# A decoder kernel: keys and values of layer 2 as three rounded products, with the low parts of the value weight in DRAM

## The chip, the cores and the metric

The kernel runs on one core of a Trainium2 chip. The metric is the device time of one execution in microseconds. A core has five engines that run side by side and wait for one another on semaphores: TensorE (PE; its weight loads are shown apart as PEld), VectorE (DVE), ScalarE (ACT), GpSimd (POOL) and SyncE (SP), which here only starts DMA transfers. Matmul results land in the eight banks of PSUM, everything else in SBUF.

## What is computed

A gated decoder of two layers on four batches of 512 rows by 512 columns. Each layer attends to a context and then runs a feed-forward part, and each part is added to the running `x` through a gate. The change touches two lines of the second layer's attention:

```python
def _L1_xattn_ref(x, cond, mask, wq, bq, wk, bk, wv, bv, wo, bo):   # 16 heads of 32
    q = _w8a8_linear(x, wq, bq)          # x and wq rounded to whole numbers up to 127
    k = cond @ wk.T + bk                 # float32, not rounded
    v = cond @ wv.T + bv                 # float32, not rounded
    attn = softmax(q k^T / sqrt(32) + mask)
    return _w8a8_linear(attn v, wo, bo)
# then: x + tanh(g) * that, and a feed-forward part (512 -> 2048 -> 512) with rounded operands
```

## The kernel before

The kernel is written engine by engine: each engine has its own list of instructions in program order, and every wait is written out. No scheduler moves anything. Layer 1 ends at about 347 us of the span, and layer 2 is the rest. Layer 2 works on one batch at a time, and all 512 rows of a batch at once: a tile is 128 rows by 512 columns, so a matrix of 512 x 512 is four tiles, and a product of two such matrices is 16 matmuls.

**Before batch 0.** TensorE turns the four weight matrices of the attention (L1393, L1400). ScalarE and VectorE copy them out of PSUM as `wqT`, `wkT` (L1255, ScalarE), `woT` (L1643) and `wvT` (L1649, VectorE). TensorE turns batch 0's context (`context`, L1420), ScalarE copies it to `ctxT` (`turned_context`, L1262), and `keys` (L1429) and `values` (L1439) multiply it by `wkT` and `wvT` as float32. Beside them VectorE normalises and rounds batch 0's rows (`query_rows`, from L57), which becomes the queries (L1455).

**High and low parts.** Scores are made from keys and queries that are each split into a rounded part and its rest: ScalarE writes `k_hi` (`key_highs`, L1267), VectorE `k_lo` (`key_lows`, L1678), and the same for `q_hi` and `q_lo` (L1297, L1721). Tiles of type F32R hold such parts. The parts are then stacked by DMA along the partitions into `k4` and `q4` (`stack_keys`, L1185, and `stack_queries`, L1196; 16 transfers for the keys of a batch, 32 for the queries). One matmul per head and row tile then gives a score (L1462). Batch 0 has transfers of its own: SP stacks the first keys (L1216), the other keys (L1222) and the last half of the queries (L1229), one after the other in SP's program; GpSimd stacks the first two quarters of the queries (L1169).

**Attention** (`attend`) goes over 64 units, a head by a row tile each, in 78 steps `s`. VectorE masks a score (L1732), ScalarE takes the exponential (L1322), TensorE turns the result (L1494), VectorE (even units) or ScalarE (odd units) copies it to `probsT` (L1762, L1313), and TensorE multiplies it by the values (L1511). `probsT` lies over the tiles that the key and query parts were made in. So the copy of unit 8, the first of the second group of eight, waits on VectorE for all stacking transfers of this batch: `k_stacked` and `q_stacked[1]`.

**The tail of a batch** is what follows the attention, and the next batch's keys and values are made in it. In program order TensorE runs: the next batch's context turned (in the last steps of the attention), two tiles of keys, the output product (L1580), two tiles of keys, three tiles of values, the turned queries, the last tile of values, the turned rows of the feed-forward part (L1410), the queries (L1455), the up product in four row tiles (L1537, each after a small matmul `hold`, L1527) and the down product (L1567). VectorE runs the row scales and rounding (L1670, L1658), the four `key_lows` between the steps of two normalisations, the values' bias (L1684), the rounding of the feed-forward rows (L1658 again), the query scaling and lows, and the hidden rows' scales. `hact`, the hidden rows that ScalarE writes (L1335), lies over `k_hi` and `k_lo`. So ScalarE waits for `k_stacked` of the next batch before it writes the first of them. Batch 3's tail has no next batch.

**Memory.** `q4` is 32 KB per partition for 16 heads; its last 8 KB are heads 12 to 15. `arena`, 32 KB, holds in turn the key parts, `ctxT`, `probsT`, `hact` and `hqT`.

## Time and profile before

| | us |
|---|---|
| median of 3 executions | 1018.43 |
| lowest and highest | 1016.8 and 1020.0 |
| the profiled execution, its own time | 1016.46 |
| its span | 1014.7 |

| engine | busy us | share of the span |
|---|---|---|
| TensorE | 899.2 | 89% |
| VectorE | 673.4 | 66% |
| ScalarE | 573.6 | 57% |
| TensorE's weight loads | 587.9 | 58% |
| GpSimd | 86.9 | 9% |

A profile is one execution seen by the hardware profiler. The span runs from the first instruction to the last. Times in the rows below are microseconds from the span's start, unless a column says ns. "SPq" is SyncE's queue issuing transfers. PEclk is the clock that TensorE was granted, as a share of 2.4 GHz; 0.5 is 1.2 GHz. The "chain of waits" is followed back from the last instruction, at each step to what released it. A float32 matmul appears as two MATMUL records, an F32R matmul as one. Records of consecutive matmuls overlap, so the pace of a stream is read from the distance of starts.

### The profile page before, as it was taken

What the parts mean: (1) busy time and instruction counts of PE and PEld (TensorE: products, weight loads), DVE (VectorE), ACT (ScalarE), POOL (GpSimd) and SP (SyncE); (2) the same over time, 40 slices, a digit from 0 to 9 for tenths busy, and PEclk for the clock granted to TensorE, in tenths of its full rate; (3) what the DMA queues carried; (4) which work ended last, traced back from release to release, by engine and by line L of the source; (5) the groups of instructions that cost most, each with busy time, mean ns of one, the idle gap of its engine ahead of it and who ended that gap; (6) DMA issues with size and microseconds to landing.
All of it is one profiled execution on the core that took longest, in us unless ns stands there. A gap on an engine that the chain in (4) does not pass through costs nothing.

```text
span 1014.7 us, 15824 instructions
## 1 busy us (share of the span) xinstructions
PE 899.2 (89%) x5592; PEld 587.9 (58%) x5592; DVE 673.4 (66%) x1870; ACT 573.6 (57%) x1094; POOL 86.9 (9%) x105
## 2 busy tenths in 40 slices
PE   3989998999999787899999999999999899999467
PEld 2868765676767453666444666445666444666233
DVE  5895860524250073798777898777798776799564
ACT  4545233355553132788347788357788447789153
POOL 2000213021120005100100000100000100000100
PEclk9999999999999999799999999999999999999769
DMA  6444556452450059510199110198110188100001
GB/s 195 141 142 159 196 205 228 146 164 86 135 198 1 23 164 197 115 43 2 42 182 191 43 43 2 42 180 186 51 43 1 43 175 196 46 2 1 1 1 42
DMA packets 52270, 102.82 MB, mean 101 GB/s; under 512 B 8924, under 2 KB 8924, under 8 KB 50656
## 3 DMA queue, kind: packets, MB, share of 16 engines
q1 hardware_dynamic: 39872, 71.88, 27.1%
q10 hardware_dynamic: 8160, 17.31, 5.1%
q0 software_dynamic: 4160, 12.62, 4.0%
q8 instruction: 45, 0.74, 0.3%
q14 instruction: 33, 0.27, 0.1%
HBM read 55.62 MB, written 14.75 MB: 69 GB/s over the span
## 4 chain that ended last, share of the span: by engine, by line
PE 36%; DVE 9%; issue 6%; ACT 5%; SPq 4%; DMA 3%; POOL 1%; POOLq 0%; DVEq 0%; ACTq 0%
PE psum L1494 7%; PE psum L1462 6%; PE psum L1567 5%; PE psum L1511 5%; PE psum L1537 5%; SPq L1185 4%; ACT probs L1322 3%; DMA k<-k_lo 3%; PE psum L1429 1%; PE psum L1553 1%; PE psum L1520 1%; DVE amax L1670 1%; DVE xn L1842 1%; DVE stats L1837 1%; DVE xn L1658 1%
## 5 line engine op out<-in xcount | busy, mean ns | idle before, releaser
L1322 ACT ACTIVATE probs<-psum,neg_max 128x512 f32<-128x512 f32 x256 | 175.0, 692 | 46.5 <-DVE neg_max L1732 46.5
L1732 DVE CUSTOM_DVE_ANT_0 psum<-psum,m_in 128x512 f32<-128x512 f32 x256 | 174.0, 703 | 18.3 <-issue 18.3
L1494 PE MATMUL psum<-ident,probs 128*128 128x128 f32 x1024 | 154.2, 275 | 0.0
L1494 PEld LDWEIGHTS psum<-ident,probs 128*128 128x128 f32 x1024 | 127.8, 141 | 19.8 <-issue 2.6
L1462 PE MATMUL psum<-k,q 128*128 128x512 f32 x256 | 125.7, 496 | 15.3 <-ACT probs L1322 6.8
L674 PE MATMUL psum<-w_sb,hT 128*128 128x512 f32 x256 | 117.6, 604 | 5.6 <-ACT hT L566 5.6
L1762 DVE COPY probsT<-psum 128x512 f32<-128x512 f32 x128 | 87.8, 686 | 2.7 <-PE psum L1494 2.5
L1313 ACT COPY probsT<-psum 128x512 f32<-128x512 f32 x128 | 75.3, 588 | 20.3 <-PE psum L1494 20.3
L594 PE MATMUL psum<-xselT_hi,w_hi 128*128 128x256 f32 x256 | 81.8, 320 | 1.6 <-ACT xselT_hi L501 1.6
L674 PEld LDWEIGHTS psum<-w_sb,hT 128*128 128x128 f32 x256 | 47.0, 192 | 55.3 <-issue 48.5
L1462 PEld LDWEIGHTS psum<-k,q 128*128 128x128 f32 x256 | 49.1, 192 | 51.7 <-ACT probs L1322 31.5
L1511 PE MATMUL psum<-probsT,vv 128*32 128x256 f32 x1024 | 68.5, 384 | 9.7 <-issue 6.1
L595 PE MATMUL psum<-xselT_lo,w_hi 128*128 128x256 f32 x256 | 71.9, 281 | 0.0
L596 PE MATMUL psum<-xselT_hi,w_lo 128*128 128x256 f32 x256 | 71.8, 281 | 0.0
L566 ACT ACTIVATE hT<-psum,b_col 128x256 f32<-128x256 f32 x64 | 26.9, 471 | 69.1 <-PE psum L596 66.5
L1162 POOL TENSOR_TENSOR xres<-xres,xn 128x512 f32<-128x512 f32 x16 | 19.8, 1268 | 531.6 <-DVE xn L1842 531.6
L1537 PE MATMUL psum<-bw1T,qxT 128*128 128x512 fp8e4 x256 | 64.4, 405 | 0.0
L1567 PE MATMUL psum<-bw2T,hqT 128*128 128x512 fp8e4 x256 | 57.1, 379 | 0.0
L1429 PE MATMUL psum<-ctxT,wkT 128*128 128x512 f32 x128 | 56.2, 593 | 0.9 <-ACT ctxT L1262 0.9
L1439 PE MATMUL psum<-wvT,ctxT 128*128 128x512 f32 x128 | 56.2, 593 | 0.0
L1335 ACT ACTIVATE hact<-psum,h_unit 128x512 f32<-128x512 f32 x64 | 41.8, 693 | 19.9 <-PE psum L1537 11.0
L594 PEld LDWEIGHTS psum<-xselT_hi,w_hi 128*128 128x128 f32 x256 | 48.3, 189 | 7.6 <-issue 5.7
(221 smaller groups left out, 1566.7 us busy)
## 6 DMA issues: line engine op xcount, KB each, us to landing
bw_raw<-in_L_ffn_W_dram ACTq DMA_DIRECT2D x16, 1024.0 KB, 5.3
c_in<-in_ctx_dram SPq DMA_DIRECT2D x8, 1024.0 KB, 5.5
k<-k_hi SPq DMA_DIRECT2D x24, 256.0 KB, 5.9
k<-k_lo SPq DMA_DIRECT2D x24, 256.0 KB, 6.7
q<-q_hi SPq DMA_DIRECT2D x48, 128.0 KB, 3.9
q<-q_lo SPq DMA_DIRECT2D x48, 128.0 KB, 3.4
xres<-in_x_dram SPq DMA_DIRECT2D x4, 1024.0 KB, 5.9
w_raw<-in_L_ffn_w_dram POOLq DMA_DIRECT2D x4, 1024.0 KB, 5.4
```

The source lines that it names most:

```text
L594: pe.matmul(dst, l_hi, r_hi, start=start, stop=False)
L595: pe.matmul(dst, l_hi, r_lo, start=False, stop=False)
L674: mm = pe.matmul(psum[j][:, :], hT[:, f % RING, j * P:(j + 1) * P], w2_sb[:, f, :], start=(f == 0), stop=(f == FT - 1))
L1313: act.copy(probsT[:, (hg + 1) % 2, r, :, (nt % 2) * P:(nt % 2) * P + P], turn_bank(u)[:, :].rearrange("p (l n) -> p l n", l=T)).then_inc(p ...
L1322: act.activation(probs[:, u % 4, :], psum[u % SCORE_BANKS][:, :], ACT.Exp, scale=-1.0, bias=neg_max[:, u:u + 1], accum_out=prob_sum[:, nt, ...
L1462: pe.matmul(psum[u % SCORE_BANKS][:, :], q4[:, h, nt * P:(nt + 1) * P], k4[:, h, :], start=True, stop=True).then_inc(score_psum, 1)
L1494: mm = pe.transpose(turn_bank(u)[:, l * P:(l + 1) * P], probs[:, u % 4, l * P:(l + 1) * P], ident[:, :])
L1511: mm = pe.matmul(psum[6 + hg % 2][HD * r:HD * (r + 1), 0:HALF], vv[:, l, h * HD:(h + 1) * HD], probsT[:, (hg + 1) % 2, r, l, :], start=(l ...
L1537: mm = pe.matmul(psum[2 + f][:, :], qxT[:, c, t * P:(t + 1) * P], bw1T[:, c, 512 * f:512 * f + 512], start=(c == 0), stop=(c == CT_ - 1))
L1567: mm = pe.matmul(psum[6 + t % 2][:, :], hqT[:, t % 2, f, :], bw2T[:, f, :], start=(f == 0), stop=(f == FT - 1))
L1732: dve.tensor_tensor_reduce(bank[:, :], bank[:, :], m_in[:, nt, :], -1.0, LOWEST, ALU.add, ALU.min, neg_max[:, u:u + 1]).then_inc(masked_re ...
L1762: dve.tensor_copy(probsT[:, (hg + 1) % 2, r, :, (nt % 2) * P:(nt % 2) * P + P], turn_bank(u)[:, :].rearrange("p (l n) -> p l n", l=T)).the ...
```

## The change

Four things are done in layer 2.

1. Context, key weight and value weight are kept as a high part of type F32R and a low part (the rest, also F32R). Each float32 matmul of `keys` and `values` becomes three F32R matmuls: high by high, high by low, low by high. ScalarE's copies now write the high parts, and VectorE subtracts them from PSUM to get the low parts: eight subtractions for the weights (where it copied `wvT` in four), and `context_lows`, four for each batch's context. ScalarE takes over the four copies of the value weight.
2. `keys` waits for the low parts too.
3. There is no room for the value weight's low part beside everything else. It is made in the last 8 KB of `q4`, stored once to DRAM (`wv_low`, 1 MB) by SP, and loaded into the same place by SP in each later batch, behind the load of `x_in`. The stacking of the second half of the queries, which writes over it, now waits for the batch's values (`v_psum`), and for the store in batch 0.
4. `attnT` and `sx_row` share 2 KB, and batch 0's context is loaded to another place.

The diff, cut to its core:

```diff
-        wkT = sb("wkT", [P, CT_, C])
-        wvT = sb("wvT", [P, CT_, C])
+        wkT_hi = sb("wkT_hi", [P, CT_, C], F32R)
+        wkT_lo = sb("wkT_lo", [P, CT_, C], F32R)
+        wvT_hi = sb("wvT_hi", [P, CT_, C], F32R)
+        wvT_lo = at("wvT_lo", [P, CT_, C], F32R, q4_at + 24 * K)
...
-        ctxT = at("ctxT2", [P, CT_, S], F32, arena + 24 * K)
+        ctxT_hi = at("ctxT2_hi", [P, CT_, S], F32R, arena + 24 * K)
+        ctxT_lo = at("ctxT2_lo", [P, CT_, S], F32R, arena + 16 * K)
...
@@ stack_queries, sync @@
+                        if half:
+                            sp.wait_ge(v_psum, b * T + T)
...
+                sp.wait_ge(linear_dve_ready, 3 * CT_)
+                sp.dma_start(wv_low, wvT_lo[:, :, :].bitcast(F32)).then_inc(wv_low_stored, 16)
                 sp.wait_ge(k_hi_ready, 1)
...
                 sp.wait_ge(q_lo_ready, CT_)
+                sp.wait_ge(v_psum, T)
+                sp.wait_ge(wv_low_stored, 16)
...
                     sp.dma_start(x_in[:, :, :], tiles(sh.x_mid[b + 1])).then_inc(x_loaded, 16)
+                    sp.dma_start(wvT_lo[:, :, :].bitcast(F32), wv_low).then_inc(wv_low_loaded, 16)
                     stack_keys(b + 1)
@@ scalar @@
-                    act.copy(wkT[:, c, :], psum[c][:, :]).then_inc(linear_act_ready, 1)
+                    act.copy(wkT_hi[:, c, :], psum[c][:, :]).then_inc(linear_act_ready, 1)
+                for c in range(CT_):
+                    act.wait_ge(linear_psum, 3 * CT_ + c + 1)
+                    act.copy(wvT_hi[:, c, :], psum[4 + c][:, :]).then_inc(linear_act_ready, 1)
@@ tensor @@
+                def three(dst, left, right, start, stop):
+                    (l_hi, l_lo), (r_hi, r_lo) = left, right
+                    pe.matmul(dst, l_hi, r_hi, start=start, stop=False)
+                    pe.matmul(dst, l_hi, r_lo, start=False, stop=False)
+                    return pe.matmul(dst, l_lo, r_hi, start=False, stop=stop)
...
-                    pe.wait_ge(ctxT_ready, b * CT_ + CT_)
+                    pe.wait_ge(ctxT_hi_ready, b * CT_ + CT_)
+                    pe.wait_ge(ctxT_lo_ready, b * CT_ + CT_)
...
-                            mm = pe.matmul(psum[4 + o][:, :], wkT[:, c, o * P:(o + 1) * P], ctxT[:, c, :],
-                                           start=(c == 0), stop=(c == CT_ - 1))
+                            mm = three(psum[4 + o][:, :], [w[:, c, o * P:(o + 1) * P] for w in (wkT_hi, wkT_lo)],
+                                       [x[:, c, :] for x in (ctxT_hi, ctxT_lo)], c == 0, c == CT_ - 1)
...
@@ vector @@
+                def context_lows(b):
+                    for c in range(CT_):
+                        dve.wait_ge(ctxT_hi_ready, b * CT_ + c + 1)
+                        dve.tensor_tensor(ctxT_lo[:, c, :], psum[CONTEXT_BANKS[c]][:, :], ctxT_hi[:, c, :].bitcast(F32),
+                                          ALU.subtract).then_inc(ctxT_lo_ready, 1)
...
                     for s in range(STEPS):
+                        if more and s == UNITS + LAG + 2:
+                            context_lows(b + 1)
...
+                context_lows(0)
                 query_rows(0, link)
```

VectorE's program before batch 0, in the kernel before. `stats` is the first step of batch 0's row normalisation.

```order
L1643 COPY woT<-psum 128x512 [waits linear_psum] x4
L1644 MEMSET turn_col 128x1
L1645 MEMSET low_col 128x1
L1646 TENSOR_SCALAR swq_col<-w_scale 128x4
L1649 COPY wvT<-psum 128x512 [waits linear_psum] x4
L1651 MEMSET held 128x1
L1652 MEMSET held 128x1
L57 BN_STATS stats<-x_in_3109 128x6 [waits x_loaded2,chain1]
```

The same place after the change.

```order
L1671 COPY woT<-psum 128x512 [waits linear_psum] x4
L1672 MEMSET turn_col 128x1
L1673 MEMSET low_col 128x1
L1674 TENSOR_SCALAR swq_col<-w_scale 128x4
L1678 TENSOR_TENSOR wkT_lo<-psum,wkT_hi 128x512 [waits linear_act_ready] x4
L1678 TENSOR_TENSOR wvT_lo<-psum,wvT_hi 128x512 [waits linear_act_ready] x4
L1681 MEMSET held 128x1
L1682 MEMSET held 128x1
L1689 TENSOR_TENSOR ctxT_lo<-psum,ctxT_hi 128x512 [waits ctxT_hi_ready2,chain1]
L1689 TENSOR_TENSOR ctxT_lo<-psum,ctxT_hi 128x512 [waits ctxT_hi_ready2] x3
L57 BN_STATS stats<-x_in_3112 128x6 [waits x_loaded2]
```

The row normalisation now stands behind the context's low parts, which wait for ScalarE's high parts.

VectorE's program in the last steps of batch 0's attention, after the change (before, the row L1689 is not there and all else is alike).

```order
L1801 COPY probsT<-psum 128x4x128 [waits pT_psum,av_psum] x2
L1807 RECIPROCAL prob_inv<-prob_sum 128x2x4 [waits probs_ready]
L1689 TENSOR_TENSOR ctxT_lo<-psum,ctxT_hi 128x512 [waits ctxT_hi_ready2] x4
L1815 TENSOR_TENSOR xn<-psum,prob_inv 128x2x128 [waits o_psum,chain2]
L1807 RECIPROCAL prob_inv<-prob_sum 128x2x4 [waits probs_ready]
L1815 TENSOR_TENSOR xn<-psum,prob_inv 128x2x128 [waits o_psum,chain2]
L1707 TENSOR_REDUCE amax<-xn 128x4 [waits o_ready]
```

The four low parts stand between the last copies of the probabilities and the last two quarters of the attention's output.

SP's program between the mask load and the first loads of batch 1, after the change. The two new transfers are L1223 and L1250; L1243 was L1229 and waited only for `q_lo_ready` and `q_hi_ready`.

```order
L1223 DMA wv_low_dram<-wvT_lo 128x2048 [waits linear_dve_ready]
L1228 DMA k_3116<-first_parts 32x512 [waits k_lo_ready,k_hi_ready]
L1228 DMA k_3116<-first_parts 32x512 x15
L1234 DMA k_3116<-k_hi_rest 32x3x512 [waits k_lo_ready,k_hi_ready]
L1234 DMA k_3116<-k_hi_rest 32x3x512 x3
L1234 DMA k_3116<-k_lo_rest 32x3x512 x4
L1234 DMA k_3116<-k_hi_rest 32x3x512 x4
L1234 DMA k_3116<-k_lo_rest 32x3x512 x4
L1243 DMA q_3117<-q_hi_rest 32x2x512 [waits v_psum,wv_low_stored,q_lo_ready,q_hi_ready]
L1243 DMA q_3117<-q_hi_rest 32x2x512 x7
L1243 DMA q_3117<-q_lo_rest 32x2x512 x8
L1185 DMA c_in_3120<-in_ctx_dram 128x4x512 [waits x_used]
L1249 DMA x_in_3112<-x_mid_dram 128x4x512 [waits ctxT_psum2]
L1250 DMA wvT_lo<-wv_low_dram 128x2048
```

The store stands ahead of all stacking transfers of batch 0, and each load behind the load of the rows.

## Rows read from the trace of the kernel before

**Rows 1.** TensorE in order of time, tail of batch 0: start us, us, operation [idle before].

```profile
486.94 7.03 PE L1429 MATMUL psum<-ctxT,wkT 128*128 128x512 f32 x16
...
507.10 10.46 PE L1439 MATMUL psum<-wvT,ctxT 128*128 128x512 f32 x24
...
522.22 1.06 PE L1410 MATMUL psum<-ident_b,xn 128*128 128x128 bf16 x16
...
534.07 0.18 PE L1527 MATMUL psum<-ident_b 128*128 128x1 bf16 x1 [3.72 <-ACT hact L1335]
```

**Rows 2.** VectorE in order of time, the same tail.

```profile
485.28 0.42 DVE L1776 TENSOR_TENSOR xn<-psum,prob_inv 128x256 f32<-128x256 f32 x1 [3.75 <-PE psum L1520]
...
487.67 2.29 DVE L1670 TENSOR_REDUCE amax<-xn 128x4 f32<-128x2048 f32 x1
...
492.92 2.46 DVE L57 BATCH_NORM_STATS2 stats<-x_in 128x6 f32<-128x512 f32 x4
...
508.02 0.75 DVE L1678 SCALAR_TENSOR_TENSOR k_lo<-psum,bk_col,k_hi 128x512 fp32r<-128x512 f32 x1
...
517.76 1.67 DVE L1658 TENSOR_SCALAR xn<-xn,inv 128x512 f32<-128x512 f32 x4
```

**Rows 3.** Queue of SP in order of time, the same tail.

```profile
483.83 0.38 SPq L1235 DMA_DIRECT2D x_in<-x_mid_dram  x1
508.85 3.54 SPq L1185 DMA_DIRECT2D k<-k_hi  x4
```

**Rows 4.** The chain of waits, the same tail: start us, us, what.

```profile
523.78 9.52 DMA k<-k_lo
...
533.33 0.70 ACT hact L1335
```

**Rows 5.** DMA issues by tile: KB of one transfer, median us from issue to landing.

```profile
x_in<-x_mid_dram SPq DMA_DIRECT2D x4, 1024.0 KB, 5.6
```

**Rows 6.** TensorE in order of time, layer 1: three-product matmuls, 24 starts apart.

```profile
60.13 0.39 PE L596 MATMUL psum<-sig_hi,ctxT_lo 128*128 128x512 f32 x1
...
65.57 0.39 PE L596 MATMUL psum<-sig_hi,ctxT_lo 128*128 128x512 f32 x1
```

**Rows 7.** VectorE, groups by line, layer 1's low parts: busy us, mean ns of one.

```profile
L824 DVE TENSOR_TENSOR ctxT_lo<-psum,ctxT_hi 128x512 fp32r<-128x512 f32 x16 | 9.9, 682 | 0.0
```

**Rows 8.** ScalarE in order of time, before batch 0's attention.

```profile
361.49 0.59 ACT L1257 COPY swo_row<-psum 128x512 f32<-128x512 f32 x1 [1.49 <-PE psum L1404]
362.82 2.05 ACT L1262 COPY ctxT<-psum 128x512 f32<-128x512 f32 x4 [0.75 <-PE psum L1420]
```

**Rows 9.** VectorE in order of time, before and in batch 0's attention.

```profile
362.16 0.69 DVE L57 BATCH_NORM_STATS2 stats<-x_in 128x6 f32<-128x512 f32 x1
...
373.74 0.74 DVE L1678 SCALAR_TENSOR_TENSOR first_parts<-psum,bk_col,first_parts 128x512 fp32r<-128x512 f32 x1
...
420.46 0.69 DVE L1762 COPY probsT<-psum 128x512 f32<-128x512 f32 x1
```

**Rows 10.** Queue of SP in order of time, before batch 0's attention.

```profile
374.55 10.14 SPq L1216 DMA_DIRECT2D k<-first_parts  x16
...
406.57 5.55 SPq L1229 DMA_DIRECT2D q<-q_lo_rest  x8
```

**Rows 11.** TensorE in order of time, batch 0's first scores.

```profile
407.57 1.62 PE L1462 MATMUL psum<-k,q 128*128 128x512 f32 x3 [6.31 <-DMA q<-first_parts]
```

**Rows 12.** Windows: start:end, length, five engines' busy us, PEclk, DMA share, GB/s.

```profile
419.00:420.00 1.00, 0.87 (x5) 0.56 (x5) 1.00 (x6) 1.00 (x4) 0.00 (x0) 1.00 0.32 59
```

**Rows 13.** Windows: the clock before and in the up products, tails of batches 0 to 2.

```profile
530.00:534.00 4.00, 0.35 (x2) 0.00 (x0) 0.23 (x1) 0.67 (x2) 0.00 (x0) 1.00 1.08 206
...
683.00:690.00 7.00, 4.73 (x18) 1.90 (x19) 4.41 (x9) 3.88 (x7) 0.00 (x0) 0.76 0.98 200
...
838.00:846.00 8.00, 7.59 (x34) 3.22 (x35) 5.77 (x10) 5.80 (x10) 0.00 (x0) 0.79 0.97 200
```

**Rows 14.** TensorE in order of time, batch 1's tail: the wait before its second up product.

```profile
685.27 0.18 PE L1527 MATMUL psum<-ident_b 128*128 128x1 bf16 x1 [2.47 <-ACT hact L1335]
```

More of the change, by code:

```diff
@@ L1071, in layer1 @@
         ctxT_psum = sem("ctxT_psum2")
[L1072 removed]
+        ctxT_hi_ready = sem("ctxT_hi_ready2")
+        ctxT_lo_ready = sem("ctxT_lo_ready2")
+        wv_low_stored = sem("wv_low_stored")
+        wv_low_loaded = sem("wv_low_loaded")
         k_psum = sem("k_psum")
@@ L1261, in turned_context @@
                         act.wait_ge(ctxT_psum, b * CT_ + c + 1)
-                        act.copy(ctxT[:, c, :], psum[CONTEXT_BANKS[c]][:, :]).then_inc(ctxT_ready, 1)
+                        act.copy(ctxT_hi[:, c, :], psum[CONTEXT_BANKS[c]][:, :]).then_inc(ctxT_hi_ready, 1)
                 def key_highs(b, tiles, k_hi=by_tile(k_hi)):
@@ L1438, in values @@
                         for c in range(CT_):
-                            mm = pe.matmul(psum[4 + t][:, :], ctxT[:, c, t * P:(t + 1) * P], wvT[:, c, :],
-                                           start=(c == 0), stop=(c == CT_ - 1))
+                            mm = three(psum[4 + t][:, :], [x[:, c, t * P:(t + 1) * P] for x in (ctxT_hi, ctxT_lo)],
+                                       [w[:, c, :] for w in (wvT_hi, wvT_lo)], c == 0, c == CT_ - 1)
                         mm.then_inc(v_psum, 1)
@@ L1646, in _ @@
                 dve.tensor_scalar(swq_col[:, :], sh.w_scale[:, 0, :], Q_SCALE, None, ALU.mult).then_inc(chain1, 1)
-                for c in range(CT_):
-                    dve.wait_ge(linear_psum, 3 * CT_ + c + 1)
-                    dve.tensor_copy(wvT[:, c, :], psum[4 + c][:, :]).then_inc(linear_dve_ready, 1)
+                for i, (w_hi, w_lo) in enumerate(((wkT_hi, wkT_lo), (wvT_hi, wvT_lo))):
+                    for c in range(CT_):
+                        dve.wait_ge(linear_act_ready, (i + 1) * CT_ + c + 1)
+                        dve.tensor_tensor(w_lo[:, c, :], psum[4 * i + c][:, :], w_hi[:, c, :].bitcast(F32),
+                                          ALU.subtract).then_inc(linear_dve_ready, 1)
                 dve.memset(held[:, 7:8], 0.0).then_inc(x_done, 1)
@@ L1653, in _ @@
                 dve.wait_ge(chain1, 3)
+                def context_lows(b):
+                    for c in range(CT_):
+                        dve.wait_ge(ctxT_hi_ready, b * CT_ + c + 1)
+                        dve.tensor_tensor(ctxT_lo[:, c, :], psum[CONTEXT_BANKS[c]][:, :], ctxT_hi[:, c, :].bitcast(F32),
+                                          ALU.subtract).then_inc(ctxT_lo_ready, 1)
                 def quantize():
@@ L1823, in batch @@
                     link.count = FIRST_LINKS
-                    attend(b, link)
+                    attend(b, link, more)
                     dve.wait_ge(o_ready, b * HG + HG)
```

20 lines of the change are left out of this document (12 added, 8 removed).

## The prediction

> **What bounds the kernel now.** I read the profile in this order: the chain of waits over layer 2, then each engine in order of time around the keys and values, then the windows with the granted clock. TensorE is the busiest engine, so less work for it looks like less time. The chain says otherwise in the places where the keys and values are made.
>
> In the tail of batch 0 VectorE starts the row scales at 487.67 [rows 2] and works without a gap that matters until the last low part of the keys at 508.02 to 508.77 [rows 2]. At 508.85 SP starts to issue the 16 key transfers [rows 3], the last of them is released at 523.78 and takes 9.52 us, and ScalarE's first hidden row starts when it has landed, at 533.33 [rows 4]. TensorE has waited 3.72 us for that by then [rows 1]. So from 487.67 to 533.33 the tail is VectorE, then SP's queue, then DMA. TensorE's matmuls lie beside them. The tails of batches 1 and 2 repeat this; batch 3's has no keys.
>
> Before batch 0 the chain does run over the keys' matmuls, but two other things stand close. VectorE normalises the rows from 362.16 and makes the first low key at 373.74 [rows 9]; SP then issues 48 stacking transfers, from 374.55 to 406.57 + 5.55 = 412.12 with hardly a gap [rows 10]. In the window 419 to 420 the DMA share falls to 0.32 [rows 12], so the last lands at about 419.3. The copy of unit 8 waits for all of them and ran at 420.46 [rows 9]. The slack is 1.2 us.
>
> **Part 1, three F32R matmuls for one float32.** Eight float32 matmuls of the keys show as 16 records; the next group starts right behind them. They took 7.03 us, about 0.87 us each [rows 1]. Layer 1 has matmuls of the same form and size, and 24 starts lie 65.57 - 60.13 = 5.44 us apart, 0.227 us each [rows 6]. A triple costs 0.68 us, so a product of 16 falls from about 13.9 to 10.9 us, and the eight products of the kernel free 24 us of TensorE.
>
> How much of it reaches the end? In a tail: the first two tiles of keys end at about 492.4 instead of 493.9. VectorE makes the first low key when it gets there, behind the rounding, and it is VectorE that is late. The second two end near 504.1, their high parts on ScalarE near 504.9, while VectorE reaches the last low key at 508.02 as before. So the transfers start at 508.85 as before. The values then end at about 516.3; the turned feed-forward rows need VectorE's rounding, 517.76 + 1.67 = 519.4 [rows 2], and start there instead of at 522.22 [rows 1]. The queries come 2.7 us earlier, and so does the first up product. All this ends in front of 533.33, which hasn't moved: TensorE waits some 6.4 us instead of 3.72. Gain of a tail: 0, bounded by 0 and the 2.7 us.
>
> A rule of the skill speaks against the exchange. The Trainium skill, in "TensorE: Matmul & The Clock Gate" under Part 3 (packing small matmuls), says that a weight load overlaps a matmul in flight only when their row groups differ. By that rule an estimate for a product is 48 x (0.227 + some 0.19 of weight load), near 20 us and dearer than before; the starts 0.227 us apart with a full-size weight load in each leave no room for it.
>
> **Part 2, low parts on VectorE.** One costs 9.9 / 16 = 0.62 us [rows 7], four of them 2.5 us. In a tail they go between VectorE's copy that ended at about 481.5 and the multiply at 485.28, where it was idle 3.75 us [rows 2]. ScalarE's four high parts end at about 484.6, so the last low part ends near 485.8 and the multiply slips 0.5 us. Its reader is the row scale at 487.67, behind a second multiply that waits for TensorE until 487.2. Cost 0; without that cover it would be 2.5 us a tail. The keys start behind a matmul at 486.94 [rows 1], later than 485.8. Cost 0.
>
> Before batch 0 there is no cover. ScalarE gets four more copies of 2.05 / 4 = 0.51 us. It was idle 1.49 us before 361.49 [rows 8], so free from 360.00, and `swo_row` moves to 362.05, 0.56 us later. The turned context waits for that PSUM bank, so the high parts of the context run from 363.38 to 365.43 [rows 8]. VectorE's low parts start at about 363.9 and end at 366.4. Only then come the row statistics, 366.4 instead of 362.16 [rows 9]: 4.25 us later. The keys end at 366.4 + 10.9 = 377.3, and VectorE arrives at the first low key at 373.74 + 4.25 = 378.0. So here too VectorE has become the later one. All four low keys are done at about 381.0, where they were done at 380.5: the queries lose 0.5 us, regain 0.7 us with the first tile of values, and the first scores [rows 11] start at 407.57 less 0.2 to 0.5.
>
> But SP's first transfer moves with the first low key, 374.55 + 4.25 = 378.8. SP is a queue with no gaps, so its last lands at 419.3 + 4.25 = 423.6. The copy of unit 8 wanted to start at 420.46; VectorE's masks queue behind it, and ScalarE and TensorE behind these. **Cost 3.1 us.** Bounds: 0, if the transfers flow faster once bunched, and 4.25 plus 1.7 for the clock after such a stop (below).
>
> **Part 3, the DRAM detour.** The store of 1 MB is issued at about 364, when SP has nothing else; it is over when the stacks start. The load goes out behind `x_in` at 483.83 [rows 3]. A transfer of that size lands 5.6 us after its issue [rows 5]: `x_in` at 489.4, needed at 492.92 [rows 2]; if the two share the engines evenly, `x_in` needs at most twice that, 495.0. Cost 0 to 2.1 us in each of three tails; I take 0, since one queue issues `x_in` first. The values need the load only at about 504. The new waits of the second half of the query stacks are for values done near 398 (batch 0) and 516 (a tail), while SP gets there at about 402 and 539. Queued behind them are the other query transfers and the mask load. Cost 0. The Trainium skill ("DMA: Bandwidth & Descriptors", on issuing engines not being separate queues) says that all transfers share the same 16 engines and interleave; by it the load could take x_in's share, which is the 2.1 us above.
>
> **Part 4, the clock.** TensorE's clock was 1.00 before the up product of batch 0's tail, after a wait of 3.72 us [rows 1, 13]. In the tail of batch 1 the wait was 2.47 us [rows 14], and the clock fell to 1.2 GHz for a while: mean 0.76 over 7 us, a loss of 0.24 x 7 = 1.7 us. The tail of batch 2 shows 0.79 over 8 us, again 1.7 us [rows 13]. TensorE bounds the up product, so this counts. After the change each tail has a wait of some 6.4 us there, and another of 3.1 us before the turned rows. I take it that batch 0's tail now loses 1.7 us like the others, and the others what they lose now: **cost 1.7 us**. Bounds: -3.4 us (no tail loses any) and +6.7 us (each loses twice 1.7).
>
> **The sum.** 1016.46 + 3.1 + 1.7 = 1021.3 us against the profiled execution. The median of the runs shown is 1018.43, 2.0 us above that execution, so for a median I say 1023.2, or 1023.
>
> **The rivals.**
> - *Neither the stacks nor the clock bite.* The transfers of batch 0 drain within the slack, the clock is as before. Nothing is on the path, the first scores gain 0.2 to 0.5 us. 1018.4, give or take 1.5. For it: the stall rests on 4.25 us against 1.2 us of slack and on a full DMA queue staying as slow.
> - *The clock bites harder.* Each tail loses 3.4 us instead of 0, 1.7, 1.7 (+6.7), and the stop in batch 0 adds 1.7 to its 3.1: 1018.4 + 11.5 = 1029.9. For it: TensorE waits twice in each tail where it waited once.
> - *Faster: the up product starts earlier.* Its place is the wait at 534.07. Were SP's key transfers or their landing bound by something that TensorE's earlier end relieves, the 2.7 us of each tail would come through: 1018.4 - 3 x 2.7 + 3.1 = 1013.4. It decides from the point where the last key transfer lands before about 527.7, when the first up product now ends. Against it: SP starts them on VectorE's last low key, at 508.85 in both.
> - *The triple is no cheaper than float32*, by the weight loads. Then a product is 6 us longer and the tails gain nothing: the keys before batch 0 end 3 us later than now, the values in a tail later too, some 12 us in all, 1030. The distance of starts [rows 6] all but excludes it.
>
> **How the numbers follow.** Forecast 0.50; rival one 0.23; harder clock 0.15; faster 0.10; dear triples 0.02. A measurement can tell about 0.3%, 3 us. The forecast's +4.8 us is over that by less than 2 us, so a fifth of its chance falls to "same", and so does part of rival one's on either side. Slower 0.40 + 0.15 + 0.02 + 0.01 = 0.58; same 0.10 + 0.20 = 0.30; faster 0.10 + 0.02 = 0.12. The range holds the forecast, rival one and most of the harder clock: 1016 to 1029.
>
> **What would show it.** VectorE's row statistics before batch 0 should start near 366.4, SP's first key transfer near 378.8, and the copy of unit 8 should wait for a DMA until about 423.6. In a tail the last low key should stand where it stood, some 21 us behind the row scales, TensorE's wait before the second up product should be about 6.4 us, and the windows there should show a clock under 1.00 in all three. If the copy of unit 8 doesn't wait, the first term is wrong; if the clock stays at 1.00, the second.

## The result, and the profile after

| | before | after |
|---|---|---|
| median of 7 executions, us | 1018.43 | 1023.9 |
| lowest and highest | 1016.8, 1021.09 | 1018.84, 1028.06 |
| the profiled execution | 1016.46 | 1021.81 |
| its span | 1014.7 | 1020.0 |

The ratio is 1.0058, with a 95% interval from 1.0039 to 1.0078: slower, by about 6 us. A second series on another chip gave 1.0068 (1.0051 to 1.0085).

The page after says that TensorE is less busy, 886.2 us instead of 899.2, and that the span is longer all the same:

```profile
PE 886.2 (87%) x5720; PEld 613.1 (60%) x5720; DVE 685.1 (67%) x1890; ACT 575.1 (56%) x1098; POOL 87.4 (9%) x105
...
PEclk9999999999999898799998999999999999999869
```

To find the place I cut layer 2 at events that both traces have, and took the differences. The times are microseconds read from the engines' rows in order of time. "Second" is a second profile of the same kernel, on another chip.

| from, to | before | second | after | second |
|---|---|---|---|---|
| layer 2's start, SP's first key transfer | 21.23 | 21.64 | 25.02 | 25.75 |
| layer 2's start, copy of unit 8 | 67.14 | 67.51 | 72.59 | 73.90 |
| copy of unit 8, row scales of batch 0's tail | 67.21 | 66.42 | 68.29 | 68.54 |
| row scales, first hidden row: tail 0 | 45.66 | 45.65 | 44.95 | 44.97 |
| the same, tail 1 | 44.40 | 44.39 | 44.40 | 44.39 |
| the same, tail 2 | 44.67 | 44.62 | 44.46 | 44.49 |
| first hidden row, next first score: tail 0 | 26.24 | 27.54 | 28.70 | 28.77 |
| the same, tail 1 | 27.91 | 27.91 | 26.25 | 26.25 |
| the same, tail 2 | 27.91 | 27.91 | 27.90 | 27.91 |
| layer 2's start, end | 656.71 | 657.52 | 662.81 | 664.53 |

The end is that of VectorE's last instruction. The attentions of batches 1 to 3 (80.6, 80.6 and 78.7 us) are equal within 0.1 us, and batch 3's tail within 0.3. So the loss lies before and in batch 0's attention: 6.5 us in the first pair and 8.5 us in the second, more than all of it in either. The three up products' stretches together are 0.8 us longer in the first pair and 0.4 us shorter in the second, so a loss there isn't shown.

**Before batch 0.** ScalarE after the change, in order of time. Columns: start us, length us, engine, line, operation, out<-in, count, [idle before <- releaser].

```profile
358.70 2.10 ACT L1273 CAST wvT_hi<-psum 128x512 fp32r<-128x512 f32 x4
360.60 0.69 ACT L1275 COPY swo_row<-psum 128x512 f32<-128x512 f32 x1
362.04 2.05 ACT L1280 CAST ctxT_hi<-psum 128x512 fp32r<-128x512 f32 x4 [0.75 <-PE psum L1445]
```

VectorE in the same place:

```profile
357.40 2.48 DVE L1678 TENSOR_TENSOR wkT_lo<-psum,wkT_hi 128x512 fp32r<-128x512 f32 x4 [0.77 <-ACT wkT_hi L1270]
359.80 2.48 DVE L1678 TENSOR_TENSOR wvT_lo<-psum,wvT_hi 128x512 fp32r<-128x512 f32 x4
...
362.72 2.49 DVE L1689 TENSOR_TENSOR ctxT_lo<-psum,ctxT_hi 128x512 fp32r<-128x512 f32 x4 [0.43 <-ACT ctxT_hi L1280]
365.12 2.46 DVE L57 BATCH_NORM_STATS2 stats<-x_in 128x6 f32<-128x512 f32 x4
...
376.71 0.75 DVE L1715 SCALAR_TENSOR_TENSOR first_parts<-psum,bk_col,first_parts 128x512 fp32r<-128x512 f32 x1
```

The four low parts (2.49 us) stand in front of the row statistics at 365.12, and they can't start before the first high part is there, at 362.72. Counted from layer 2's start (353.32 before, 352.51 after) the statistics moved from 8.84 to 12.61, the first low key from 20.42 to 24.20: 3.8 us each [rows 9], and 4.1 us in the second pair. ScalarE's four copies of the value weight, which the prediction charged with 0.56 us, moved nothing in this pair: `swo_row` starts 8.09 us behind layer 2's start instead of 8.17, and the context's high parts 9.53 instead of 9.50 [rows 8]. In the second pair `swo_row` starts 0.3 us later. SP's queue follows:

```profile
377.53 10.12 SPq L1228 DMA_DIRECT2D k<-first_parts  x16
...
412.79 5.15 SPq L1243 DMA_DIRECT2D q<-q_lo_rest  x8
```

ScalarE and VectorE at unit 8, the first in each row with the wait in brackets:

```profile
425.09 0.58 ACT L1331 COPY probsT<-psum 128x512 f32<-128x512 f32 x1 [4.70 <-DMA q<-q_lo_rest]
425.10 0.69 DVE L1801 COPY probsT<-psum 128x512 f32<-128x512 f32 x1 [5.55 <-issue]
```

The last query transfer was issued at 417.35 and landed 7.7 us later, at 425.0. ScalarE waited 4.70 us, VectorE 5.55, which before had no wait there [rows 9]. But before it was a close thing. The last query transfer in the kernel before, its issue at 411.51 and its time to landing:

```profile
L1229 SPq DMA_DIRECT2D q<-q_lo_rest x1: 599/599/599, 411.5 to 411.5; - x1
...
DMA to landing us min/median/max: 8.8/8.8/8.8
```

It landed at 420.3, 0.1 us before the copy of unit 8 at 420.46. In the second profile of the kernel before it landed at 420.45, and VectorE had to wait for it:

```profile
420.52 0.69 DVE L1762 COPY probsT<-psum 128x512 f32<-128x512 f32 x1 [0.70 <-issue]
```

So the kernel before had no slack here, and the delay of SP's queue reaches unit 8 in full. After the stop TensorE ran on a lower clock. Windows: start:end, length, busy us of TensorE, its weight loads, VectorE, ScalarE, GpSimd, then PEclk, DMA share, GB/s.

```profile
420.00:425.00 5.00, 1.97 (x15) 1.38 (x11) 0.00 (x0) 0.39 (x2) 0.00 (x0) 0.97 0.74 136
425.00:430.00 5.00, 3.75 (x21) 2.38 (x25) 4.59 (x15) 3.91 (x10) 0.00 (x0) 0.50 0.00 0
430.00:435.00 5.00, 4.65 (x36) 2.97 (x32) 3.38 (x14) 2.84 (x7) 0.00 (x0) 0.85 0.00 0
```

**In the first tail.** VectorE, then SP, ScalarE and TensorE, after the change:

```profile
488.88 2.48 DVE L1689 TENSOR_TENSOR ctxT_lo<-psum,ctxT_hi 128x512 fp32r<-128x512 f32 x4 [1.62 <-ACT ctxT_hi L1280]
491.28 0.42 DVE L1815 TENSOR_TENSOR xn<-psum,prob_inv 128x256 f32<-128x256 f32 x1
...
493.39 2.29 DVE L1707 TENSOR_REDUCE amax<-xn 128x4 f32<-128x2048 f32 x1
513.77 0.73 DVE L1715 SCALAR_TENSOR_TENSOR k_lo<-psum,bk_col,k_hi 128x512 fp32r<-128x512 f32 x1
```

```profile
489.99 1.74 SPq L1250 DMA_DIRECT2D wvT_lo<-wv_low_dram  x1
514.59 3.58 SPq L1193 DMA_DIRECT2D k<-k_hi  x4
```

```profile
510.48 0.69 ACT L1285 ACTIVATE k_hi<-psum,bk_col 128x512 fp32r<-128x512 f32 x1 [2.11 <-PE psum L1412]
...
538.34 2.42 ACT L1353 ACTIVATE hact<-psum,h_unit 128x512 f32<-128x512 f32 x4 [5.70 <-DMA k<-k_lo]
```

```profile
525.06 1.05 PE L1435 MATMUL psum<-ident_b,xn 128*128 128x128 bf16 x16 [2.04 <-DVE xn L1695]
...
539.08 0.19 PE L1555 MATMUL psum<-ident_b 128*128 128x1 bf16 x1 [5.73 <-ACT hact L1353]
```

The low parts fit into VectorE's idle time. The last high key ends at 511.17, but VectorE reaches the last low key at 513.77, 20.38 us behind the row scales; before it was 20.35 [rows 2]. TensorE has two waits now, 2.04 us for the rounded rows (none before) and 5.73 us for the first hidden row (3.72 before [rows 1]). In tails 1 and 2 the second wait is 3.51 and 3.81 us (2.47 [rows 14] and 2.74 before). There the clock falls early, behind the first of the two waits (in tail 2 once more behind the second); tail 1, TensorE behind the wait and then a window:

```profile
679.25 1.05 PE L1435 MATMUL psum<-ident_b,xn 128*128 128x128 bf16 x16 [2.03 <-DVE xn L1695]
```

```profile
681.00:684.00 3.00, 3.00 (x9) 1.04 (x8) 1.04 (x2) 1.74 (x3) 0.00 (x0) 0.50 1.07 203
```

TensorE is slower in this place but still comes before the keys' transfers, so this fall costs nothing. The DRAM load is issued behind `x_in`, and no engine waits for either.

### The profile page after: what moved, and what is told of

The parts are those of the page before. It is cut to its first block, busy times and chain, and to the rows that moved or that the text cites. A ratio compares the mean times of both kernels' runs of the same rounds, so it can differ in the third digit from the quotient of the medians.

```text
span 1020.0 us, 16116 instructions
## 1 busy us (share of the span) xinstructions
PE 886.2 (87%) x5720; PEld 613.1 (60%) x5720; DVE 685.1 (67%) x1890; ACT 575.1 (56%) x1098; POOL 87.4 (9%) x105
## 4 chain that ended last, share of the span: by engine, by line
PE 32%; DVE 11%; SPq 8%; issue 6%; ACT 5%; DMA 3%; POOL 0%; POOLq 0%; DVEq 0%; ACTq 0%
PE psum L1522 7%; PE psum L1490 6%; PE psum L1595 5%; PE psum L1539 5%; PE psum L1565 5%; SPq L1193 4%; ACT probs L1340 3%; DMA k<-k_lo 2%; SPq L1234 2%; PE psum L1581 1%; DVE amax L1707 1%; SPq L1243 1%; DVE stats L57 1%; SPq L1228 1%; PE psum L1548 1%
## 5 line engine op out<-in xcount | busy, mean ns | idle before, releaser
L1340 ACT ACTIVATION_READ_ACCUMULATOR probs<-psum,neg_max 128x1 f32 x256 | 52.5, 205 | 0.0
L595 PEld LDWEIGHTS psum<-xselT_lo,w_hi 128*128 128x128 f32 x256 | 48.2, 188 | 5.7 <-issue 5.7
```

The lines of the kernel that those rows point to most:

```text
L595: pe.matmul(dst, l_hi, r_lo, start=False, stop=False)
L1340: act.activation(probs[:, u % 4, :], psum[u % SCORE_BANKS][:, :], ACT.Exp, scale=-1.0, bias=neg_max[:, u:u + 1], accum_out=prob_sum[:, nt, ...
```

## The experiments

Every kernel was profiled. Times of segments are from layer 2's start unless said otherwise. The first four kernels below ran once each, 1025.29, 1024.16, 1022.38 and 1019.60 us, with 1021.38 us for the kernel before beside them. Single executions of the changed kernel lie between 1018.8 and 1028.1 us, so these four tell nothing by their times and are read by their segments.

### One product instead of three

```diff
-                    pe.matmul(dst, l_hi, r_hi, start=start, stop=False)
-                    pe.matmul(dst, l_hi, r_lo, start=False, stop=False)
-                    return pe.matmul(dst, l_lo, r_hi, start=False, stop=stop)
+                    return pe.matmul(dst, l_hi, r_hi, start=start, stop=stop)
```

> The changed kernel with one matmul (high by high) in place of three in all keys and values of layer 2; the low parts are still made, stored and loaded, only not multiplied, so keys and values are only as good as the high parts. TensorE does 256 matmuls of 0.23 us less, about 15 us in each of the three tails. Theory (VectorE, SP's queue and DMA bound the tails): the row scales to the first hidden row stay at 44.4 to 45.0 us in each tail, SP's first key transfer stays 25.0 us behind layer 2's start, and the execution changes only by the clock, within 3 us. Rival (TensorE's work in keys and values reaches the end): each tail gets shorter by several us, 10 us or more in all.

Measured: row scales to first hidden row: 45.00, 45.62 and 44.42 us. SP's first key transfer at 25.69, the copy of unit 8 at 73.13. VectorE and ScalarE in the first tail:

```profile
495.40 2.29 DVE L1705 TENSOR_REDUCE amax<-xn 128x4 f32<-128x2048 f32 x1
...
515.75 0.73 DVE L1713 SCALAR_TENSOR_TENSOR k_lo<-psum,bk_col,k_hi 128x512 fp32r<-128x512 f32 x1
510.00 0.69 ACT L1285 ACTIVATE k_hi<-psum,bk_col 128x512 fp32r<-128x512 f32 x1 [0.24 <-PE psum L1410]
...
540.40 2.42 ACT L1353 ACTIVATE hact<-psum,h_unit 128x512 f32<-128x512 f32 x4 [4.71 <-DMA k<-k_lo]
```

The last low key stands 20.35 us behind the row scales, as it does with three products. Tail 1 came out 0.6 us above the expected range: its last key transfer landed later after SP had started at the same place. Some 15 us of TensorE's work less in each tail brought nothing. The rival falls: TensorE's keys and values don't reach the end of a tail.

### Batch 0 without the context's low parts

```diff
-                            mm = three(psum[4 + o][:, :],
+                            mm = (three if b else one)(psum[4 + o][:, :],
...
-                context_lows(0)
                 query_rows(0, link)
```

(`one` multiplies high by high; `values` has the same edit, and `keys` of batch 0 doesn't wait for low parts.)

> The changed kernel where batch 0 alone leaves out its context's four low parts on VectorE and multiplies high by high only, so batch 0's keys and values are only as good as the high parts. Theory (VectorE's four low parts in front of batch 0's row statistics delay SP's stacking queue): SP's first key transfer comes 2.9 us earlier, 22.1 us behind layer 2's start instead of 25.0, and the copy of unit 8 some 3 us earlier, 69.6 instead of 72.6; the tails stay as they are. Rival (the stop at unit 8 comes from the DMA engines, not from SP's start): the copy of unit 8 moves by less than 1 us.

Measured: SP's first key transfer at 22.30, 2.7 us earlier, and the copy of unit 8 at 69.10, 3.5 us earlier than in the first profile of the changed kernel and 4.8 earlier than in the second. Layer 2's start to batch 0's row scales took 137.6 us, against 140.9 and 142.4 with the change and 134.4 and 133.9 without. The theory holds and the rival falls, with a reservation: the edit also takes two thirds of the matmuls out of batch 0's keys and values, so the first scores come 3.5 us earlier too. It is not the whole loss: between the first score (50.85) and the copy of unit 8 there are still 18.3 us, where the kernel before takes 12.9. The first scores come 3.4 us earlier here than in the kernel before, while SP's queue still starts 1.1 us later than there.

### Batch 0's low parts twice

```diff
                 context_lows(0)
+                for c in range(CT_):
+                    dve.tensor_tensor(xn[:, c, :], ctxT_hi[:, c, :].bitcast(F32), ctxT_hi[:, c, :].bitcast(F32), ALU.subtract)
                 query_rows(0, link)
```

> The changed kernel where VectorE does four more subtractions of the same size (into a tile that is overwritten later) behind batch 0's context low parts: 2.5 us more on VectorE before batch 0's row statistics, nothing else. Theory: SP's first key transfer at 27.5 us behind layer 2's start instead of 25.0, the copy of unit 8 at 75.1 instead of 72.6, the whole 2.5 us longer. Rival (DMA bound): the copy of unit 8 moves by less than 1 us.

Measured: SP's first key transfer at 27.61, 2.6 us later, as expected. The copy of unit 8 at 74.07, only 1.5 us later than in the first profile of the changed kernel and 0.2 later than in the second (73.90), and from there to the row scales 66.43 us instead of 68.29, so batch 0 was not longer at all (140.5 us to the row scales, against 140.9). Half of the expectation is a miss. The windows of this kernel show where the first scores went (TensorE's clock is the number before the DMA share):

```profile
376.00:381.00 5.00, 2.08 (x9) 1.31 (x8) 4.89 (x12) 0.69 (x2) 0.00 (x0) 0.92 0.01 3
381.00:386.00 5.00, 3.01 (x21) 2.63 (x22) 0.58 (x1) 2.71 (x3) 0.00 (x0) 0.50 0.44 102
386.00:391.00 5.00, 5.00 (x14) 1.79 (x13) 1.59 (x3) 1.44 (x2) 0.00 (x0) 0.55 0.45 105
```

TensorE waited 3.55 us for the last low key, then turned rows and made queries at 1.2 GHz. So the first score came at 60.06, 5.7 us later. ScalarE's wait for the transfers at unit 8 shrank to 0.88 us, and the clock didn't fall behind it. In this profile the late first scores and the stop lay over one another and weren't added. The run doesn't tell what a further delay of SP's queue costs, because the first scores moved as well.

### Without the DRAM detour

```diff
-                sp.wait_ge(linear_dve_ready, 3 * CT_)
-                sp.dma_start(wv_low, wvT_lo[:, :, :].bitcast(F32)).then_inc(wv_low_stored, 16)
...
-                    sp.dma_start(wvT_lo[:, :, :].bitcast(F32), wv_low).then_inc(wv_low_loaded, 16)
```

> The changed kernel without the store of the value weight's low part to DRAM and without the three loads; the values of batches 1 to 3 multiply by the high part a second time where they multiplied by the low part, so they are wrong and their cost is the same. Theory: the detour is hidden, all segments stay within 0.3 us apart from the clock. Rival (the load takes DMA time from the load of the rows): the row scales to the first hidden row get up to 2 us shorter in the tails.

Measured: row scales to first hidden row 44.96, 44.41 and 44.55 us, against 44.95, 44.40 and 44.46 with the detour. SP's first key transfer at 25.43, the copy of unit 8 at 72.17. In the tails the detour costs nothing. Before batch 0 the two changed profiles with the store stand at 72.60 and 73.90 at unit 8, a spread of 1.3 us, and the 72.17 here lies just under it, so a cost there is not told. The first scores were 1.9 us later here, at 56.30, ScalarE's wait at unit 8 was 2.46 us instead of 4.70, and the clock stayed at 1.00 behind it, so that it took 66.42 us to the row scales instead of 68.29.

### SP's order: high parts first

The stop and the tails have one thing in common: SP waits for the last low key before it issues anything. Half of its transfers copy high parts only.

```diff
                     sp.wait_ge(k_hi_ready, b * CT_ + CT_)
-                    sp.wait_ge(k_lo_ready, b * CT_ + CT_)
-                    for g, part in enumerate((k_hi, k_lo, k_hi, k_lo)):
+                    for g, part in ((0, k_hi), (2, k_hi), (1, k_lo), (3, k_lo)):
+                        if g == 1:
+                            sp.wait_ge(k_lo_ready, b * CT_ + CT_)
```

(and the same for batch 0's first quarter.)

> The changed kernel with one change in SP's order: of the 16 key transfers of a stack the eight that copy high parts go first and wait for the high parts alone, the eight of the low parts follow and wait for the low parts; in batch 0 (first quarter) and in the three tails. Theory (the stacks' start bounds both places, and TensorE's earlier keys were of no use because VectorE's last low key came late): in the tails SP starts when the last high key is there, 3.4 us earlier, so row scales to first hidden row about 41.5 us instead of 44.4 to 45.0; before batch 0 SP starts 18 us behind layer 2's start instead of 25, and the copy of unit 8 at 67.5 instead of 72.6. In all some 15 us less than the changed kernel, near 1008, faster than both. Rival (DMA engines bound the stacks): the tails gain under 1 us.

Measured: 1003.52 us, ratio to the kernel before 0.986 (0.983 to 0.989). It beats both kernels, and by more than the expected 1008. Row scales to first hidden row 41.11, 40.90 and 42.48 us, up stretches 26.25, 26.25 and 28.96; SP's first key transfer at 17.92, the copy of unit 8 at 67.06. In the first tail:

```profile
505.42 0.69 ACT L1287 ACTIVATE k_hi<-psum,bk_col 128x512 fp32r<-128x512 f32 x1 [2.11 <-PE psum L1414]
506.13 7.81 SPq L1194 DMA_DIRECT2D k<-k_hi  x8
508.72 0.73 DVE L1717 SCALAR_TENSOR_TENSOR k_lo<-psum,bk_col,k_hi 128x512 fp32r<-128x512 f32 x1
529.44 4.31 ACT L1355 ACTIVATE hact<-psum,h_unit 128x512 f32<-128x512 f32 x7 [1.85 <-DMA k<-k_lo]
```

SP starts at 506.13, right behind the last high key, 17.80 us behind the row scales (488.33) instead of 21.20, and no longer waits for VectorE's 508.72. Tail 1 starts at 17.80 too, tail 2 at 19.48: there TensorE ran the keys in part at 1.2 GHz (0.50 in the window 792 to 795), and the last high key came 1.7 us later. With the old order such a fall costs nothing, because VectorE's low key is later still: in tail 1 of the kernel with matmuls in the wait (below) the last high key came at the same late place, and SP started 21.2 us behind the row scales all the same.

### The same order in the kernel before

> The kernel before with the same change in SP's order. Theory: there the last high key ends at 508.0 and the last low key at 508.8, so a tail gains only 0.8 us, and batch 0, where unit 8 did not wait, gains nothing: some 2 us in all. Rival (the order by itself is the gain, whatever TensorE does): as much as in the changed kernel.

The edit is the one above, made in the kernel before. Measured: 1009.12 us, ratio 0.992 (0.990 to 0.994). The expected 2 us were too few. Row scales to first hidden row 43.94, 43.18 and 43.33 us, 1.2 to 1.7 less each; the copy of unit 8 at 66.18, 1 us less.

```profile
509.31 0.69 ACT L1269 ACTIVATE k_hi<-psum,bk_col 128x512 fp32r<-128x512 f32 x1 [2.75 <-PE psum L1431]
510.03 7.83 SPq L1186 DMA_DIRECT2D k<-k_hi  x8
510.03 0.75 DVE L1680 SCALAR_TENSOR_TENSOR k_lo<-psum,bk_col,k_hi 128x512 fp32r<-128x512 f32 x1
```

The start moved as forecast, from 21.2 to 20.3 us behind the row scales in each tail. Another 0.4 to 0.9 us came after it: from SP's first key transfer to the first hidden row it took 23.60, 22.85 and 23.00 us instead of 24.48, 23.23 and 23.5. What I left out is the clock. The waits before the second up product are 2.01, 1.26 and 1.40 us here instead of 3.72, 2.47 and 2.74, and all three up stretches ran at full clock in this profile (26.25, 26.25 and 26.24 us), 3.3 us less than in the first profile of the kernel before.

On top of the new order the change itself is now worth 1009.1 - 1003.5 = 5.6 us by the medians of four executions each (1008.4 to 1011.0 and 1001.2 to 1006.5). In the tails SP waits for the last high key, and that one hangs on TensorE's product: SP starts 20.3 us behind the row scales with float32 keys and 17.8 us with the three rounded products (19.5 in one tail of three). Here the cheaper product comes through.

### The new order in batch 0 alone

> The changed kernel with the new order of SP for batch 0's first quarter alone. Theory: the copy of unit 8 at 67.5 us behind layer 2's start instead of 72.6, no stop, and with it no lower clock behind it; tails as in the changed kernel. 5 to 6 us less than the changed kernel, level with the kernel before within 2 us.

Measured: 1017.10 us, ratio to the kernel before 0.9995 (0.998 to 1.001). SP's first key transfer at 17.06, the copy of unit 8 at 68.55, 1 us later than expected, with 0.77 us of waiting on VectorE instead of 5.55. From there it took 66.42 us to the row scales, the clock at 1.00; tails 45.00, 44.46 and 45.78. The changed kernel's two series stand 0.6% and 0.7% above the kernel before, so this took back the 6 to 7 us. The loss of the change is in batch 0, and it hangs on when SP's queue starts. (SP starts here even earlier than in the kernel before, whose unit 8 gained 1 us from the same order. So the time alone doesn't say that the loss is gone to the last microsecond.)

### Matmuls in TensorE's wait

```diff
                     up(b, 0, more)
+                    if more:
+                        for i in range(20):
+                            pe.matmul(psum[0][:, :], qxT[:, 0, 0:P], woT[:, 0, :], start=True, stop=True)
                     up(b, 1)
```

> The changed kernel with 20 matmuls more in each of the three tails, of which nobody reads the result, between the first and the second up product, where TensorE waits some 5.7 us for the first hidden row. Theory (part of the loss is TensorE's clock after this wait): the clock stays at 1.00 and each tail from the first hidden row to the next batch's first score takes 26.24 us, where the changed kernel's profile shows 28.70, 26.25 and 27.90; 4 us less in all. Rival (the clock is not the cause): these stretches keep their 26 to 29 us.

Measured: 1020.33 us, ratio 1.0033 (1.0019 to 1.0047), against 1.0058 and 1.0068 for the changed kernel. First hidden row to next first score 26.24 us in all three tails. The clock of the changed kernel in 8 us from the first hidden row, tails 0 to 2:

```profile
538.00:546.00 8.00, 6.92 (x26) 2.71 (x27) 4.41 (x9) 5.17 (x8) 0.00 (x0) 0.61 1.07 203
692.00:700.00 8.00, 7.25 (x43) 3.45 (x44) 6.97 (x12) 7.01 (x11) 0.00 (x0) 1.00 1.07 202
843.00:851.00 8.00, 7.01 (x31) 2.93 (x32) 5.20 (x10) 5.74 (x9) 0.00 (x0) 0.79 1.07 201
```

and of this one:

```profile
539.00:547.00 8.00, 6.96 (x40) 3.27 (x41) 6.70 (x11) 6.86 (x11) 0.00 (x0) 1.00 1.08 203
692.00:700.00 8.00, 7.34 (x44) 3.53 (x45) 7.02 (x12) 6.96 (x12) 0.00 (x0) 1.00 1.08 202
844.00:852.00 8.00, 7.60 (x44) 3.32 (x42) 6.69 (x10) 6.82 (x11) 0.00 (x0) 1.00 1.07 201
```

PEclk is 0.61, 1.00 and 0.79 in the first and 1.00 in all of the second. The mechanism holds: the clock falls because of the wait, and the stretch pays for it. Its price is 82.85 - 78.72 = 4.1 us over the three stretches of the profiles. By the ratios it is 2.5 to 3.6 us of the kernel's time, but the intervals of the first comparison overlap (1.0047 against 1.0039). Part of the difference lies before the stretches: row scales to first hidden row took 45.02, 45.80 and 45.60 us here, 2.6 us more in sum, since the last key transfers landed later. Tails without extra matmuls show such landings too (45.62 with one product, 45.78 with the new order in batch 0 alone); their cause is open.

### The changed kernel and the kernel before again

> The changed kernel once more, beside the two runs below on the same chip. A second profile of it shows which of its segments repeat. Theory: SP's first key transfer 25.0 us behind layer 2's start, the stop before the copy of unit 8 again (71.5 to 73), the tails to the first hidden row 44.4 to 45.8 us; the up products' stretches 26.25 us at full clock or 27.9 to 29 after a fall, differing from profile to profile. Rival (one of these was chance of the first profile): no stop at unit 8.

> The kernel before once more. Theory: no stop at unit 8 (66.5 to 67.5 us behind layer 2's start), the stretches from the first hidden row to the next first score again 26.24 or 27.9 us, in tails that may differ from those of the first profile.

Measured: 1023.67 us (ratio 1.0068, 1.0051 to 1.0085) and 1016.97 us. Their segments are the "second" columns above. The stop at unit 8 is there again, ScalarE's wait 4.96 us. The kernel before was not free of it as expected: VectorE waited 0.70 us there. In the seven profiles that have the change, SP's old order in the tails and no extra matmuls, tail 0 always fell (28.5 to 29.1 us), tail 1 in three of seven, tail 2 in five of seven. Chance is not all of it. In each of the six tails that stayed at full clock behind the first hidden row, the clock had already fallen in or behind the wait for the rounded rows, so TensorE came later to the second wait and stood there for 3.2 to 3.5 us. In the fifteen tails that fell, some of them for a second time, this wait was 3.8 to 6.6 us. In the kernel before, which has no first wait, waits of 2.5 to 2.7 us were enough four times out of four, and 3.72 us once out of twice. So the length of the wait alone doesn't tell either.

### Both: high parts first, and matmuls in the wait

The edits of the two experiments together, with eight matmuls instead of 20.

> The changed kernel with SP's new order (high parts first) and eight matmuls without a reader in each tail's wait before the second up product. With the order alone one of three tails lost 2.7 us to the clock in its profile and two lost nothing. Theory: all three stretches at 26.24 us, about 1 us less in the mean than with the order alone, near 1002.5. Rival: the eight matmuls hide nothing or come late, no gain or 1 to 2 us more.

Measured: 1003.21 us, ratio 0.987 (0.985 to 0.989). It can't be told from the order alone (0.986). Up stretches 26.24, 27.73 and 26.24 us. The long one in tail 1 is not the clock's doing. TensorE, ScalarE and a window there:

```profile
676.50 1.89 PE L1633 MATMUL psum<-woT,qxT 128*128 128x512 bf16 x8
675.99 2.42 ACT L1355 ACTIVATE hact<-psum,h_unit 128x512 f32<-128x512 f32 x4
676.00:684.00 8.00, 8.00 (x45) 3.67 (x43) 6.19 (x11) 6.10 (x10) 0.00 (x0) 1.00 0.85 188
```

The clock is at 1.00. It had fallen before, behind the wait for the rounded rows (0.50 in the window 668 to 671), so TensorE came so late that nothing was left of the second wait, and the eight matmuls stood in the way of an up product whose hidden row was ready at 675.99. That is the rival's "come late". With the order alone two of three tails stay at full clock as well, so these matmuls show no gain.

## Why the prediction was right, step by step

The forecast was 1023 us, slower, in a range from 1016 to 1029. The median was 1023.9. The direction and the places follow from the mechanism; that the number is so close is luck, since two errors of opposite sign nearly cancel (see the sum).

- **TensorE's saving is hidden.** Right. Layer 1 shows 5.44 us for 24 starts [rows 6]; keys in the changed kernel run 0.233 us apart at full clock (starts at 492.90 and 498.03, 22 apart). So a product of 48 takes 11.2 us, and the rival of dear triples is out. Tails to the first hidden row: expected as before, measured -0.71, 0.00 and -0.21 us. Leaving out two thirds of the products gained nothing (one product instead of three).
- **VectorE's low parts before batch 0.** Right in mechanism, a little too large: SP's start was put 4.25 us later and came 3.8 us later, 4.1 in the second pair. What was too much is the 0.56 us for ScalarE's copies: `swo_row` and the context's high parts didn't move in the first pair.
- **The stop at unit 8.** The place was right, the size too small. Forecast 3.1 us, measured 5.45 us (67.14 to 72.59) and 6.4 us in the second pair. Two steps were off. The first is the slack of 1.2 us. It came from a DMA share of 0.32 in one window [rows 12], read as a last landing at 419.3; the transfer itself landed at 420.3, and the slack was 0.1 us. The second is that I shifted the landing rigidly with SP's start. From SP's first key transfer to the last landing it took 45.8 us before, in both profiles, and 47.5 and 48.1 us after. So the 5.45 us are 3.8 of later start and 1.7 of slower transfers, with nothing taken off. The windows over this stretch, the changed kernel's, which ends 0.5 us before the last landing, and then the one of before, which ends 0.8 us before it (columns as above, GB/s last):

```profile
377.53:424.53 47.00, 30.81 (x163) 22.28 (x161) 21.14 (x55) 17.95 (x37) 15.71 (x32) 0.85 0.86 179
```

```profile
374.55:419.55 45.00, 34.09 (x126) 19.11 (x125) 20.30 (x51) 16.95 (x34) 15.72 (x32) 0.89 0.87 187
```

Why the engines moved less per microsecond is open. One difference stands in the rows: GpSimd's share starts 14.2 us behind SP's in the changed kernel and 18.5 us before. Whether that makes the 1.7 us no run here shows.

- **The clock behind the stop.** I had it as a bound (1.7 us) and took 0. From unit 8 to the row scales it cost 1.1 us, and 2.1 in the second pair. Over all profiles it is near 2 us: behind a shorter wait at unit 8 (0.7 to 3.3 us on VectorE) the clock stayed up and it took 66.4 us in the second profile of the kernel before and in four of the experiments, and behind the full stop (4.8 to 5.8 us) 68.2 to 68.7 us in five profiles. The first profile of the kernel before had no wait there and took 67.21, and the new order in the kernel before, without a wait as well, 67.27.
- **The clock in the tails.** Right that tail 0 would fall; the rest was off. Forecast 1.7 us, measured +2.46, -1.66 and -0.01: 0.8 us in the first pair, and -0.4 us in the second, since the second profile of the kernel before shows tail 0 falling as well (27.54). The wait before the second up product was put at 6.4 us in each tail; it was 5.73, 3.51 and 3.81. The step that failed is that tails 1 and 2 would keep what they lose. I counted the new wait before the turned rows (2.0 us, forecast 3.1) as one more reason to fall, but behind it a fall is free and shortens the second wait, as tail 1 shows.
- **The DRAM detour.** Right in the tails: 0. Before batch 0 it is not told apart from the spread between profiles.
- **The sum.** 5.45 + 1.1 - 0.9 + 0.8 - 0.3 (batch 3) = 6.1 us in layer 2, against 4.8. Layer 1, which the change doesn't touch, was 0.8 us shorter in the profiled execution. So two errors partly cancelled: the stop too cheap by 3.4 us with its clock, the tails' clock too dear by 0.9 and the tails' small gains left out. In the second pair the stop with its clock is 8.5 us, 5.4 more than forecast, and the tails' clock 2.1 less.

## What to carry to other kernels

Before making the busiest engine's work cheaper, look at who releases the next transfer or the next buffer, and what the cheaper form puts on that engine; here the rounded products freed some 19 us of TensorE (an estimate from the starts in the first tail's keys, 0.86 us for a float32 matmul and 0.71 us for three rounded ones, times 128), and low parts on VectorE, ahead of a queue that was only just in time, cost 6. Read slack from the landing of the last transfer, not from a falling DMA share. When a queue waits for two products, issue first what needs only the earlier one: this was worth 8 us without the change and made the change worth 5.6. And a stop of a few microseconds can be paid a second time where TensorE bounds what follows, as a lower clock: 1 to 2 us behind unit 8.

## What the runs showed of the hardware

- Rounded matmuls (F32R, 128 x 512) with a new weight tile each run 0.227 us apart in layer 1 and 0.233 us in layer 2 at 2.4 GHz, with weight loads of 0.19 us each beside them; in batch 0's keys of the changed kernel, where the clock was at 0.52 (window 366.5 to 370), 0.43 us apart (starts 367.37 to 367.80).
- TensorE's clock fell behind a wait of 2.47 us [rows 14] and behind one of 2.03 us (tail 1 of the changed kernel), but not behind each: 3.72 us of waiting left it at 1.00 in one profile of the kernel before, and in the second profile the same tail lost 1.3 us. Twenty matmuls in the wait of 5.7 us left 1.50 us of it, and the clock stayed at 1.00 in all three up stretches.
- The same 16 key transfers: from SP's first one to the first hidden row it took 23.2 to 24.6 us in the old order and 22.9 to 23.6 with all high parts first. So the order gains mainly by the start, 0.8 us a tail in the kernel before and 3.4 us in the changed one, and by a few tenths in the transfers.
- Batch 0's stacking transfers took 45.8 us from SP's first transfer to the last landing in both profiles of the kernel before (184 GB/s), and 47.5 and 48.1 us in the changed kernel's (178 and 175 GB/s).
